# Twenty-four layer norms of a two-layer decoder: where the residual is added, where the statistics are read and which engine applies them

## The chip, the cores and the metric

One core of one Trainium2 chip runs the whole program in one launch. The metric is the device time of that launch in microseconds (us). TensorE (PE) multiplies and writes its results to PSUM. VectorE (DVE) and ScalarE (ACT) read PSUM and SBUF, GpSimd (POOL) reads SBUF, and SyncE (SP) issues the transfers. Each engine works through its own instructions in order and waits on semaphores for the others.

## The reference

The input is two sequences of 1024 tokens with 256 features. Two decoder layers follow, each with three sublayers, and after each sublayer stands a layer norm without affine terms:

```
def _layernorm(x, axis=-1, eps=1e-05):
    m = jnp.mean(x, axis=axis, keepdims=True)
    v = jnp.var(x, axis=axis, keepdims=True)
    return (x - m) / jnp.sqrt(v + eps)

x = _layernorm(x + _L0_attn_ref(...))    # recurrent mixer (scan over 1024 steps), then 32 -> 256
x = _layernorm(x + _L0_xattn_ref(...))   # cross attention to 77 context rows, 16 heads
x = _layernorm(x + _L0_ffn_ref(...))     # entmax-gated experts, 256 -> 1024 -> 256
x = _layernorm(x + _L1_attn_ref(...))    # self attention, 16 heads of 64
x = _layernorm(x + _L1_xattn_ref(...))   # cross attention
x = _layernorm(x + _L1_ffn_ref(...))     # blockwise FP4 gate/up/down, 256 -> 704 -> 256
```

All arithmetic of the norms is in float32.

## The kernel before

The program runs in stages one after the other: `project` and `scan` (the recurrent mixer), `first_layer` (its stage name is `one`), `self_attention` (`self`), and `second_layer` (`two`). The norms stand in `first_layer` and `second_layer` alone.

Both layers are tiled alike. A group is 256 tokens of each of the two sequences; there are four groups, and each engine loops over them by itself, without a barrier between groups. One sequence is one `Chain`, called chain 0 and chain 1 here; it has four PSUM banks of its own and works on two token tiles of 128 (`CTILES = 2`). Each part of a layer is written as a generator for each engine, and `in_turns` takes one step of chain 0, then one step of chain 1, and so on. That fixes the order of the instructions on every engine: a step ends where the code says `yield`, usually just before a wait. Since both chains run the same code, the order is always step i of chain 0, step i of chain 1, step i+1 of chain 0. An engine that waits in a step of chain 1 therefore also holds back the next step of chain 0.

A sublayer ends in products on PE that leave the sublayer's output in a PSUM bank, `y(j)` with 256 columns for token tile j, and a semaphore `y_ready` after the last of the two tiles:

- norm 1 of layer one: line 1114, one product per tile (`wout` by `sqg`)
- norm 2 of both layers: lines 832 and 833, two products with 128 rows each per tile, and one product with a single row that adds the bias `bo`
- norm 3 of layer one: line 976, one product per tile
- norm 1 of layer two: line 1923, eight products per tile (`wo` by `aT`)
- norm 3 of layer two: line 1806, six products per tile, the last with 64 rows

Every such float32 product with 256 columns shows in the trace as two MATMUL records and two LDWEIGHTS records. A transpose (`pe.transpose`, lines 643, 799, 1773, 1799) of 128 columns shows as one.

Class `Norm` (lines 588 to 628) then does, for each chain: DVE adds the residual to the bank and writes x to SBUF (608, two instructions); DVE takes statistics of x (611, two), aggregates them (614, two) and adds epsilon (616, one); POOL raises the variance to the power -0.5 (628, one); DVE subtracts the mean and multiplies (620, two). Each of these is a step of its own, or nearly so. In norm 1 DVE waits ahead of that for `stored`, the store of the last group's x, and for `in_loaded`, the load of the residual `xin`; in norms 2 and 3 the residual is x itself.

After the norms of layer one and after norm 1 of layer two, `Flip` transposes x on PE into bank 2 (643) and copies it to `xT` on ACT (653). After norm 2 of layer two, DVE quantises x (`quantise`, lines 1737 to 1746), and PE transposes the result (1773). After norm 3, SP stores x (1162, 1962). The bias and the query projections are applied by ACT with the same kind of instruction that the change uses (842: `ACT.Identity` with a bias from SBUF).

## Time and profile before

| | |
|---|---|
| Median of three runs | 3557.69 us (3557.44 to 3558.20) |
| The profiled execution's own time | 3557.47 us |
| Its span (first to last instruction) | 3555.5 us |
| PE busy | 2047.1 us (58%) |
| PE weight loads | 1173.9 us (33%) |
| DVE busy | 2272.2 us (64%) |
| ACT busy | 1768.2 us (50%) |
| POOL busy | 611.8 us (17%) |
| Mean granted TensorE clock | 0.70 |

Busy shares are means over the whole program. The stages have different limits: layer one runs from about 1505 to 1990 us of the span and layer two from about 3000 to its end, and a change to the norms can be worth something only there. The granted clock is given as a share of 2.4 GHz: 0.50 is 1.2 GHz, 1.00 is 2.4 GHz.

### The profile page before, as it was taken

The page shows a single profiled execution, that of the slowest core. Times are in us where ns is not written, and L with a number is a line of the kernel's source. Part 1 is how long each engine was busy: PE and PEld are TensorE (multiplying, and loading weights), DVE is VectorE, ACT ScalarE, POOL GpSimd, SP SyncE. Part 2 cuts the span into 40 slices and gives each one's busy share as a digit, 9 for nine tenths or more (in the row PEclk, how much of TensorE's full clock was granted, in tenths as well). Part 3 has the DMA queues.
Part 4 walks back from the last instruction along what each step waited for, and adds up shares of the span by engine and source line. Part 5 has one row for each costly group of instructions (what it writes and reads, how often), then busy time and mean ns, then how long its engine had stood idle before and what let it go on. Part 6 is the DMA issues. An engine that isn't in the chain of part 4 may idle for free. (4 is left out here: it accounts for less than half of the span.)

```text
span 3555.5 us, 43628 instructions
## 1 busy us (share of the span) xinstructions
PE 2047.1 (58%) x10084; PEld 1173.9 (33%) x10084; DVE 2272.2 (64%) x10243; ACT 1768.2 (50%) x5640; POOL 611.8 (17%) x335
## 2 busy tenths in 40 slices
PE   5322222322322222377676599999999983777776
PEld 3222222222222222244443333333333322454453
DVE  3699999999999999743434244554444545444445
ACT  2388888888888888422221244444444441221221
POOL 0000000000000000000000056666666660000000
PEclk8655555555555555567666799999999995777787
DMA  3322222222222222200000100000000002010000
GB/s 80 81 58 53 65 54 52 61 57 53 56 62 53 52 66 52 69 12 24 24 10 1 40 11 14 9 13 16 13 13 9 13 15 81 30 36 6 29 6 6
DMA packets 87805, 129.52 MB, mean 36 GB/s; under 512 B 17572, under 2 KB 64712, under 8 KB 87368
## 3 DMA queue, kind: packets, MB, share of 16 engines
q1 hardware_dynamic: 87624, 127.76, 14.6%
q14 instruction: 147, 1.20, 0.1%
q8 instruction: 34, 0.56, 0.1%
HBM read 103.58 MB, written 23.10 MB: 36 GB/s over the span
## 5 line engine op out<-in xcount | busy, mean ns | idle before, releaser
L541 PE MATMUL scan_acc<-mixer_qbd,scan_flat 128*128 128x4 f32 x1024 | 228.8, 355 | 886.4 <-ACT scan_flat L502 886.4
L513 ACT ACTIVATE scan_cand<-scan_state,scan_cbuf 128x32 f32<-128x32 f32 x2048 | 647.8, 316 | 35.5
L516 ACT ACTIVATE scan_cand<-scan_pre,scan_cbuf 128x32 f32<-128x32 f32 x2048 | 589.0, 288 | 137.8
L1582 DVE TENSOR_REDUCE self_tops<-self_rough 128x2 f32<-128x1024 f32 x256 | 311.5, 1217 | 461.5 <-PE self_rough L1364 461.5
L446 DVE SCALAR_TENSOR_TENSOR scan_prod<-scan_keys,scan_cbuf,scan_cand 128x65 f32<-128x65 f32 x2048 | 585.6, 286 | 18.1 <-issue 8.5
L461 DVE SCALAR_TENSOR_TENSOR scan_pre<-scan_keys,scan_gap,scan_state 128x32 f32<-128x32 f32 x2048 | 527.7, 258 | 36.1
L541 PEld LDWEIGHTS scan_acc<-mixer_qbd,scan_flat 128*128 128x128 f32 x1024 | 223.2, 330 | 912.1 <-ACT scan_flat L502 912.1
L452 DVE SCALAR_TENSOR_TENSOR scan_state<-scan_cand,scan_cbuf 128x32 f32<-128x32 f32 x2048 | 505.0, 247 | 0.0
L1568 POOL TENSOR_TENSOR self_psum<-self_psum,self_prob 128x1024 f32<-128x1024 f32 x192 | 451.2, 2350 | 161.2 <-ACT self_prob L1494 151.8
L628 POOL TENSOR_TENSOR one_norm_rstd<-one_norm_var,one_half 128x2 f32<-128x2 f32 x24 | 18.0, 768 | 1920.0 <-DVE one_norm_var L616 1920.0
L1494 ACT ACTIVATE self_prob<-self_sco 128x1024 f32<-128x1024 f32 x256 | 261.5, 1024 | 137.9 <-PE self_sco L1377 129.3
L1373 PE MATMUL self_sco<-self_qk 64*128 64x512 f32 x1024 | 279.5, 623 | 26.4 <-DMA self_w<-in_w_qkv 22.8
L1388 PE MATMUL self_out<-self_prob,self_v 128*64 128x512 f32 x1024 | 248.8, 607 | 0.0
L532 PE MATMUL scan_flip<-all_ident,scan_state 128*128 128x128 f32 x520 | 126.1, 424 | 100.8 <-DVE scan_state L452 100.8
L446 DVE DVE_READ_ACCUMULATOR scan_prod<-scan_keys,scan_cbuf,scan_cand 128x1 f32 x2048 | 168.9, 82 | 0.0
L502 ACT ACTIVATE scan_flat<-scan_flip 128x128 f32<-128x128 f32 x520 | 138.7, 268 | 1.6 <-PE scan_flip L532 1.6
L1333 PE MATMUL self_misc<-self_xT,self_w 128*128 128x512 f32 x256 | 128.7, 626 | 18.6 <-DMA self_xT<-xT_rows 15.1
L532 PEld LDWEIGHTS scan_flip<-all_ident,scan_state 128*128 128x128 f32 x520 | 101.9, 223 | 105.1 <-DVE scan_state L452 85.9
L1600 DVE RECIPROCAL self_rden<-self_den 128x128 f32<-128x128 f32 x128 | 119.7, 939 | 23.8 <-ACT self_den L1504 23.8
L1373 PEld LDWEIGHTS self_sco<-self_qk 64*128 64x128 f32 x1024 | 93.2, 191 | 116.5 <-issue 101.5
L653 ACT ACTIVATE one_xT<-one_bank 128x512 f32<-128x512 f32 x24 | 14.3, 597 | 229.9 <-PE one_bank L643 229.9
L1485 ACT ACTIVATE self_qk<-self_misc 128x512 f32<-128x512 f32 x64 | 38.2, 597 | 169.1 <-PE self_misc L1333 169.1
(376 smaller groups left out, 3116.4 us busy)
## 6 DMA issues: line engine op xcount, KB each, us to landing
scan_keys<-k_rows SPq DMA_DIRECT2D x260, 260.0 KB, 4.8
aT_rows<-self_aT SPq DMA_DIRECT2D x32, 256.0 KB, 2.4
two_aT<-aT_rows SPq DMA_DIRECT2D x8, 1024.0 KB, 8.0
scan_cbuf<-coef_rows SPq DMA_DIRECT2D x65, 80.0 KB, 5.4
coef_rows<-proj_coef SPq DMA_DIRECT2D x4, 1280.0 KB, 6.0
self_w<-in_w_qkv SPq DMA_DIRECT2D x8, 384.0 KB, 3.5
k_rows<-proj_krow SPq DMA_DIRECT2D x32, 65.0 KB, 3.6
proj_xin<-in_xT SPq DMA_DIRECT2D x8, 256.0 KB, 3.2
```

Source lines behind the costliest of these rows:

```text
L446: dve.scalar_tensor_tensor(prod[:, b, :], keys[:, h, b, s_, :], coef(NIB, h, s_, b), cand[:, b, s % 2, :], ALU.mult, ALU.mult, accum_out=g ...
L452: dve.scalar_tensor_tensor(state[:, h, s_, b, :], cand[:, b, s % 2, 0:NS], weight, cand[:, b, s % 2, NS:2 * NS], ALU.mult, ALU.add).then_i ...
L461: dve.scalar_tensor_tensor(pre[:, b, 0:NS], keys[:, h, b, s_, NS:2 * NS], gap[:, b:b + 1], state[:, hp, sp_, b, :], ALU.mult, ALU.add).the ...
L513: act.activation(cand[:, b, (s + 1) % 2, NS:2 * NS], state[:, hp, sp_, b, :], ACT.Copy, scale=cbuf[:, h, KEEP, b, s_:s_ + 1]).then_inc(kep ...
L516: act.activation(cand[:, b, (s + 1) % 2, 0:NS], pre[:, b, 0:NS], ACT.Tanh, scale=cbuf[:, h, BETA, b, s_:s_ + 1]).then_inc(c_ready[b], 1)
L532: mm = pe.transpose(flip[:, i // 4, (i % 4) * P:(i % 4 + 1) * P], state[:, h, 2 * i:2 * i + 2, :, :].rearrange("p s b j -> p (s b j)"), id ...
L541: mm = pe.matmul(acc[:, at // 512, at % 512:at % 512 + 4], flat[:, i, :], qbd[:, at:at + 4], start=True, stop=True)
L1373: pe.matmul(sco[:, kt % 2, u, :], qk[rows, b, 1, kt * P:(kt + 1) * P], qk[rows, b, 0, hf * HALF:(hf + 1) * HALF], start=True, stop=False)
L1388: mm = pe.matmul(out[u * AD:(u + 1) * AD, :], v[:, b, kt, u, :], prob[:, kt, u, :], start=(kt == 0), stop=(kt == NQ - 1))
L1494: act.activation(prob[:, kt, :, :], sco[:, kt % 2, :, :], ACT.Exp, scale=AD ** -0.5).then_inc(p_ready, 1)
L1568: pool.tensor_tensor(psum[:, hf, :, :], before, prob[:, kt, :, :], ALU.add).then_inc(summed, 1)
L1582: dve.tensor_reduce(tops[:, kh, t, :], rough[:, :, :], AX.X, ALU.max).then_inc(rough_taken, 1)
```

## The change

The residual is no longer added by DVE. PE adds it in the bank: after a tile's products comes one more, `ident` (the 128 by 128 identity) by x of that tile, into the same `y(j)`. PE waits for `in_loaded` in place of DVE. DVE takes its statistics from the bank, and after POOL's power it computes `low` = -mean * rstd in one instruction of two columns. ACT then writes x = rstd * y + low from the bank, two instructions per chain. The wait for the last store moves from DVE to ACT. ACT's list of parts gets the three norms; for each chain a norm's step stands ahead of the flip's.

```
 class Norm:
-    LINKS = 3
+    LINKS = 2
...
+        self.low = ch.sb(name + "_low", [P, CTILES])
...
     def dve(self, dve, g):
         link = ChainLinks(dve, self.links, self.LINKS, g)
-        if self.free:
-
-            yield
-            dve.wait_ge(self.free, g * 16 + 16)
         yield
         dve.wait_ge(self.y_ready, g + 1)
         for j in range(CTILES):
-            ins = dve.tensor_tensor(self.x[:, j, :], self.src[:, j, :], self.ch.y(j, self.bank), ALU.add)
-        yield from link(ins)
-        for j in range(CTILES):
-            ins = dve.bn_stats(self.stats[:, j, :], self.x[:, j, :])
+            ins = dve.bn_stats(self.stats[:, j, :], self.ch.y(j, self.bank))
         yield from link(ins, (self.y_ready, 1))
         for j in range(CTILES):
             ins = dve.bn_aggr(self.mv[:, j, :], self.stats[:, j, :])
...
         dve.tensor_scalar(self.var[:, :], self.mv[:, :, 1], LN_EPS, None, ALU.add).then_inc(self.var_ready, 1)
         yield
         dve.wait_ge(self.rstd_ready, g + 1)
+        dve.scalar_tensor_tensor(self.low[:, :], self.mv[:, :, 0], -1.0, self.rstd[:, :], ALU.mult, ALU.mult).then_inc(self.low_ready, 1)
+        link.close()
+
+    def act(self, act, g):
+        if self.free:
+
+            yield
+            act.wait_ge(self.free, g * 16 + 16)
+        yield
+        act.wait_ge(self.low_ready, g + 1)
         for j in range(CTILES):
-            ins = dve.tensor_scalar(self.x[:, j, :], self.x[:, j, :], self.mv[:, j, 0:1], self.rstd[:, j:j + 1],
-                                    ALU.subtract, ALU.mult)
+            ins = act.activation(self.x[:, j, :], self.ch.y(j, self.bank), ACT.Identity, bias=self.low[:, j:j + 1], scale=self.rstd[:, j:j + 1])
         ins.then_inc(self.ready, 1)
-        link.close()
...
 # CrossAttention.pe (norm 2, both layers)
-            mm = pe.matmul(self.ch.y(j), w.ones[0:1, 0:P], w.bvo[:, 1, :], start=False, stop=True)
+            pe.matmul(self.ch.y(j), w.ones[0:1, 0:P], w.bvo[:, 1, :], start=False, stop=False)
+            mm = pe.matmul(self.ch.y(j), w.ident[:, :], x[:, j, :], start=False, stop=True)
...
 # EntmaxFFN.pe (norm 3, layer one)
-            mm = pe.matmul(self.ch.y(j), self.zT[:, 1, j * P:(j + 1) * P], w.o2[:, :], start=True, stop=True)
+            pe.matmul(self.ch.y(j), self.zT[:, 1, j * P:(j + 1) * P], w.o2[:, :], start=True, stop=False)
+            mm = pe.matmul(self.ch.y(j), self.ident[:, :], x[:, j, :], start=False, stop=True)
...
 # first_layer: Sublayers.pe (norm 1)
                 pe.wait_ge(bo_ready, g + 1)
+                pe.wait_ge(self.in_loaded, g * 16 + 16)
                 for j in range(CTILES):
...
+                    mm = pe.matmul(self.ch.y(j), ident[:, :], self.xin[:, j, :], start=False, stop=True)
...
             def act(self, act, g):
-                for part in (self.flip1, self.xa, self.flip2, self.ff, self.flip3):
+                for part in (self.norm1, self.flip1, self.xa, self.norm2, self.flip2, self.ff, self.norm3, self.flip3):
                     yield from part.act(act, g)
...
             def dve(self, dve, g):
-                yield
-                dve.wait_ge(self.in_loaded, g * 16 + 16)
...
 # Fp4FFN.pe (norm 3, layer two)
+            mm = pe.matmul(self.ch.y(j), w.ident[:, :], x[:, j, :], start=False, stop=True)
...
 # second_layer: Sublayers.pe (norm 1)
                 pe.wait_ge(self.a_loaded, g * 16 + 16)
+                pe.wait_ge(self.in_loaded, g * 16 + 16)
...
+                    mm = pe.matmul(self.ch.y(j, 0), ident[:, :], self.xin[:, j, :], start=False, stop=True)
...
             def act(self, act, g):
-                for part in (self.flip1, self.xa, self.ff):
+                for part in (self.norm1, self.flip1, self.xa, self.norm2, self.ff, self.norm3):
                     yield from part.act(act, g)
```

## Rows read from the trace of the kernel before

**Rows 1.** The page's slices: busy tenths and granted clock, 89 us each.
```profile
PE   5322222322322222377676599999999983777776
DVE  3699999999999999743434244554444545444445
ACT  2388888888888888422221244444444441221221
PEclk8655555555555555567666799999999995777787
```

**Rows 2.** The chain that ended last, layer two, first group: start, us, engine, output, line.
```profile
3068.76 1.15 PE two_bank L833 x2
3069.90 2.01 PE two_bank L832 x4
3071.91 1.16 PE two_bank L833 x2
3073.09 0.75 DVE two_x L608 x2
...
3077.18 0.73 DVE two_x L620 x2
3078.42 0.67 DVE two_q_amax L1737
...
3085.33 1.97 PE two_bank L1773 x8
...
3138.60 14.03 PE two_bank L1923 x64
...
3261.82 13.18 PE two_bank L1806 x48
3274.99 14.03 PE two_bank L1923 x64
```

**Rows 3.** Timeline, norm 1 of layer one, second group: start, us, engine, line, tiles.
```profile
1630.89 3.78 PE L1114 MATMUL one_bank<-one_wout,one_sqg 128*128 128x256 f32 x8 [8.65 <-DVE one_sqg L1221]
...
1634.70 0.75 DVE L608 TENSOR_TENSOR one_x<-one_xin,one_bank 128x256 f32<-128x256 f32 x2 [0.86 <-PE one_bank L1114]
1635.37 1.40 DVE L611 BATCH_NORM_STATS2 one_norm_stats<-one_x 128x6 f32<-128x256 f32 x4
1636.69 0.43 DVE L614 BATCH_NORM_AGGREGATE one_norm_mv<-one_norm_stats 128x2 f32<-128x6 f32 x4
1637.04 0.28 DVE L616 TENSOR_SCALAR one_norm_var<-one_norm_mv 128x2 f32<-128x2 f32 x2
1637.26 1.49 POOL L628 TENSOR_TENSOR one_norm_rstd<-one_norm_var,one_half 128x2 f32<-128x2 f32 x2 [17.01 <-DVE one_norm_var L616]
1637.99 1.54 DVE L620 TENSOR_SCALAR one_x<-one_x,one_norm_mv,one_norm_rstd 128x256 f32<-128x256 f32 x4 [0.66 <-POOL one_norm_rstd L628]
...
1638.77 1.97 PE L643 MATMUL one_bank<-all_ident,one_x 128*128 128x128 f32 x8 [4.11 <-DVE one_x L620]
```

**Rows 4.** Timeline, norm 3 of layer one, second group.
```profile
1735.77 1.89 PE L976 MATMUL one_bank<-one_ff_o,one_ff_zT 128*128 128x256 f32 x8
...
1736.83 1.61 DVE L608 TENSOR_TENSOR one_x<-one_x,one_bank 128x256 f32<-128x256 f32 x4 [0.38 <-PE one_bank L976]
...
1741.76 1.92 PE L643 MATMUL one_bank<-all_ident,one_x 128*128 128x128 f32 x8 [4.10 <-DVE one_x L620]
```

**Rows 5.** Timeline, norm 1 of layer two, second group, and its release by PE.
```profile
3138.53 14.08 PE L1923 MATMUL two_bank<-two_wo,two_aT 128*128 128x256 f32 x64
...
3142.86 1.19 SPq L1962 DMA_DIRECT2D out<-two_x  x2
3146.06 0.75 DVE L608 TENSOR_TENSOR two_x<-two_xin,two_bank 128x256 f32<-128x256 f32 x2 [2.61 <-DMA out<-two_x]
3152.64 0.75 DVE L608 TENSOR_TENSOR two_x<-two_xin,two_bank 128x256 f32<-128x256 f32 x2 [5.83 <-PE two_bank L1923]
```

**Rows 6.** Timeline, the end of the program.
```profile
3548.04 0.75 DVE L608 TENSOR_TENSOR two_x<-two_x,two_bank 128x256 f32<-128x256 f32 x2 [5.21 <-PE two_bank L1806]
...
3551.31 1.54 DVE L620 TENSOR_SCALAR two_x<-two_x,two_norm_mv,two_norm_rstd 128x256 f32<-128x256 f32 x4 [0.65 <-POOL two_norm_rstd L628]
```

**Rows 7.** Groups by form on ACT: busy us, mean ns of one, idle before.
```profile
L653 ACT ACTIVATE one_xT<-one_bank 128x512 f32<-128x512 f32 x24 | 14.3, 597 | 229.9 <-PE one_bank L643 229.9
...
L842 ACT ACTIVATE one_xa_q<-one_bank,one_xa_bqk 128x256 f32<-128x256 f32 x16 | 6.7, 479 | 0.0
...
L846 ACT ACTIVATE one_xa_topT<-one_bank 128x256 f32<-128x256 f32 x8 | 3.1, 384 | 36.0 <-PE one_bank L799 35.8
```

**Rows 8.** Groups by form on DVE in layer one: busy us, mean ns, idle before.
```profile
L620 DVE TENSOR_SCALAR one_x<-one_x,one_norm_mv,one_norm_rstd 128x256 f32<-128x256 f32 x44 | 16.1, 409 | 8.0 <-POOL one_norm_rstd L628 7.2
...
L611 DVE BATCH_NORM_STATS2 one_norm_stats<-one_x 128x6 f32<-128x256 f32 x44 | 15.3, 411 | 0.0
...
L608 DVE TENSOR_TENSOR one_x<-one_x,one_bank 128x256 f32<-128x256 f32 x32 | 12.0, 417 | 47.7 <-PE one_bank L833 45.7 <-PE one_bank L976 1.5
...
L616 DVE TENSOR_SCALAR one_norm_var<-one_norm_mv 128x2 f32<-128x2 f32 x22 | 3.1, 153 | 0.0
```

**Rows 9.** Windows of 1.5 us: busy time of each engine; PEclk is the granted clock.
```profile
3060.00:3061.50 1.50, 1.12 (x3) 0.94 (x4) 0.92 (x2) 0.00 (x0) 0.00 (x0) 0.50 0.00 0
3072.00:3073.50 1.50, 1.06 (x2) 0.34 (x2) 0.41 (x2) 0.00 (x0) 0.00 (x0) 0.50 0.00 0
...
3085.50:3087.00 1.50, 1.50 (x8) 1.40 (x8) 0.38 (x1) 0.52 (x1) 0.00 (x0) 0.50 0.00 0
3090.00:3091.50 1.50, 1.50 (x5) 0.72 (x4) 0.00 (x0) 0.00 (x0) 0.00 (x0) 0.91 0.00 0
...
1643.00:1644.50 1.50, 1.50 (x9) 1.32 (x8) 0.00 (x0) 0.70 (x2) 0.00 (x0) 0.99 0.50 193
```

More of the change, by code:

```diff
@@ L588, with __init__ @@
 class Norm:
-    LINKS = 3
-    def __init__(self, ch, name, src, x, y_ready, half, free=None, bank=3):
-        self.ch, self.src, self.x, self.y_ready, self.half, self.free, self.bank = ch, src, x, y_ready, half, free, bank
+    LINKS = 2
+    def __init__(self, ch, name, x, y_ready, half, free=None, bank=3):
+        self.ch, self.x, self.y_ready, self.half, self.free, self.bank = ch, x, y_ready, half, free, bank
         self.stats = ch.sb(name + "_stats", [P, CTILES, 6])
         self.mv, self.rstd, self.var = ch.sb(name + "_mv", [P, CTILES, 2]), ch.sb(name + "_rstd", [P, CTILES]), ch.sb(name + "_var", [P, CTILES])
-        self.var_ready, self.rstd_ready, self.ready, self.links = (
-            ch.sem(name + "_var_ready"), ch.sem(name + "_rstd_ready"), ch.sem(name + "_ready"), ch.sem(name + "_links"))
+        self.low = ch.sb(name + "_low", [P, CTILES])
+        self.var_ready, self.rstd_ready, self.low_ready, self.ready, self.links = (
+            ch.sem(name + "_var_ready"), ch.sem(name + "_rstd_ready"), ch.sem(name + "_low_ready"), ch.sem(name + "_ready"),
+            ch.sem(name + "_links"))
     def dve(self, dve, g):
         link = ChainLinks(dve, self.links, self.LINKS, g)
-        if self.free:
-            yield
-            dve.wait_ge(self.free, g * 16 + 16)
         yield
@@ L932, in __init__, with pe @@
             sem("h_made"), sem("h_ready"), sem("z2_made"), sem("z2_ready"), sem("y_ready"), sem("links"))
-    def pe(self, pe, g, xT, x_flipped):
+    def pe(self, pe, g, x, xT, x_flipped):
         w, banks = self.w, self.ch.banks
@@ L1098, in __init__ @@
                     ch.sem("in_loaded"), ch.sem("y_ready"), ch.sem("stored"), ch.sem("xT_stored"))
-                self.norm1 = Norm(ch, "norm1", self.xin, self.x, self.y_ready, half, self.stored)
+                self.norm1 = Norm(ch, "norm1", self.x, self.y_ready, half, self.stored)
                 self.flip1 = Flip(ch, "flip1", self.x, self.norm1.ready, self.xT, ident, self.xT_stored)
                 self.xa = CrossAttention(ch, context)
-                self.norm2 = Norm(ch, "norm2", self.x, self.x, self.xa.y_ready, half)
+                self.norm2 = Norm(ch, "norm2", self.x, self.xa.y_ready, half)
                 self.flip2 = Flip(ch, "flip2", self.x, self.norm2.ready, self.xT, ident)
                 self.ff = EntmaxFFN(ch, experts, ident, half)
-                self.norm3 = Norm(ch, "norm3", self.x, self.x, self.ff.y_ready, half)
+                self.norm3 = Norm(ch, "norm3", self.x, self.ff.y_ready, half)
                 self.flip3 = Flip(ch, "flip3", self.x, self.norm3.ready, self.xT, ident)
@@ L1765, in __init__, with pe @@
             sem("hq_ready"), sem("h_flipped"), sem("hT_ready"), sem("y_ready"), sem("links"))
-    def pe(self, pe, g):
+    def pe(self, pe, g, x):
         w, banks = self.w, self.ch.banks
@@ L1805, in pe @@
                 size = min(P, FI - r * P)
-                mm = pe.matmul(self.ch.y(j), self.hqT[0:size, j, r, :], w.wdT[0:size, r, :], start=(r == 0), stop=(r == self.FT - 1))
+                pe.matmul(self.ch.y(j), self.hqT[0:size, j, r, :], w.wdT[0:size, r, :], start=(r == 0), stop=False)
+            mm = pe.matmul(self.ch.y(j), w.ident[:, :], x[:, j, :], start=False, stop=True)
         mm.then_inc(self.y_ready, 1)
@@ L1909, in __init__ @@
                     ch.sem("in_loaded"), ch.sem("a_loaded"), ch.sem("y_ready"), ch.sem("stored"))
-                self.norm1 = Norm(ch, "norm1", self.xin, self.x, self.y_ready, half, self.stored, bank=0)
+                self.norm1 = Norm(ch, "norm1", self.x, self.y_ready, half, self.stored, bank=0)
                 self.flip1 = Flip(ch, "flip1", self.x, self.norm1.ready, self.xT, ident)
                 self.xa = CrossAttention(ch, context)
-                self.norm2 = Norm(ch, "norm2", self.x, self.x, self.xa.y_ready, half)
+                self.norm2 = Norm(ch, "norm2", self.x, self.xa.y_ready, half)
                 self.ff = Fp4FFN(ch, fp4)
-                self.norm3 = Norm(ch, "norm3", self.x, self.x, self.ff.y_ready, half)
+                self.norm3 = Norm(ch, "norm3", self.x, self.ff.y_ready, half)
             def pe(self, pe, g):
@@ L1919, in pe @@
                 pe.wait_ge(self.a_loaded, g * 16 + 16)
+                pe.wait_ge(self.in_loaded, g * 16 + 16)
                 for j in range(CTILES):
                     for c in range(CT):
-                        mm = pe.matmul(self.ch.y(j, 0), self.aT[:, c, j * P:(j + 1) * P], wo[:, c, :], start=(c == 0), stop=(c == CT - 1))
+                        pe.matmul(self.ch.y(j, 0), self.aT[:, c, j * P:(j + 1) * P], wo[:, c, :], start=(c == 0), stop=False)
+                    mm = pe.matmul(self.ch.y(j, 0), ident[:, :], self.xin[:, j, :], start=False, stop=True)
                 mm.then_inc(self.y_ready, 1)
                 yield from self.flip1.pe(pe, g)
-                yield from self.xa.pe(pe, g, self.xT, self.flip1.ready)
-                yield from self.ff.pe(pe, g)
+                yield from self.xa.pe(pe, g, self.x, self.xT, self.flip1.ready)
+                yield from self.ff.pe(pe, g, self.x)
             def act(self, act, g):
-                for part in (self.flip1, self.xa, self.ff):
+                for part in (self.norm1, self.flip1, self.xa, self.norm2, self.ff, self.norm3):
                     yield from part.act(act, g)
@@ L1937, in dve @@
             def dve(self, dve, g):
-                yield
-                dve.wait_ge(self.in_loaded, g * 16 + 16)
                 yield from self.norm1.dve(dve, g)
```

10 lines of the change are left out of this document (5 added, 5 removed).

## The prediction

> **What bounds the kernel now.** I read the page's slices first, to see in which stages the norms stand: no engine is full there (DVE 3 to 5 tenths, PE 7 to 8, ACT 1 to 4), and PE's granted clock is between its two levels [rows 1]. Two chains take turns and each waits for the other engine, so the time of these stages is the length of a chain of waits. The chain that ended last comes next: in layer two it runs through PE's last products for chain 1, then DVE's addition, statistics, POOL's power, DVE's scaling, and on to the quantiser [rows 2]. Between groups it goes over the products of lines 1806 and 1923, which stand back to back on PE [rows 2]. So PE's products ahead of a norm are on the path, all of them, and those of both chains, since chain 1's come after chain 0's. Then the timeline of one norm of each kind, to time each link of it [rows 3 to 6].
>
> Call Y the moment when chain 1's bank is complete (DVE's addition for chain 1 begins). Before, in norm 1 of layer one, Y = 1634.70 and the flip on PE begins at 1638.77: Y + 4.07 [rows 3].
>
> **What is added on PE.** Four identity products per norm (two chains, two tiles), of 256 columns: two records each, so 8 records. At full clock line 1923's 64 records take 14.08, one 0.22 [rows 5]; at 1.2 GHz twice that, 0.43 to 0.44, and line 1114's eight agree (3.78 in all, with the tail of the last) [rows 3]. So 8 records cost 1.75 at full clock and 3.45 at the lower.
> A change between 128-row and one-row products costs more: lines 832 and 833 take 2.0 + 1.15 = 3.15 for six records [rows 2], 0.54 more than 6 x 0.435, with two changes per tile, so 0.27 each. The identity product puts one more such change at the end of norm 2.
> Its bounds: a product as cheap as two transposes, which show one record per 128 columns [rows 3] (half of the above), up to the 0.57 per record of line 833 (4.6 for eight) [rows 2].
>
> **What leaves DVE, and what ACT takes.** After Y, DVE no longer adds, and chain 0's statistics are already done: they wait no more behind chain 1's addition. From Y: chain 1's statistics, two instructions 0.33 apart (four take 1.40 [rows 3], one 0.411 [rows 8]), 0.66; aggregation 0.35; to POOL's start 0.22: POOL begins at Y + 1.23, before at Y + 2.56. The power and its hand-over 0.73 (1637.26 to 1637.99), so DVE's small instruction stands at Y + 1.96. It takes 0.16, like others of two columns (0.153 [rows 8]), and 0.09 to hand over: ACT begins at Y + 2.21. ACT's form with one operand from SBUF took 0.479 for 256 columns, without one 0.384 [rows 7]: an operand costs 0.095, and with a scale from SBUF too I take 0.57. A pair takes about 1.0, so chain 0's x is ready at Y + 3.2 and the flip starts at Y + 3.27. Saved: 0.8. Bounds for the pair: 0.75 (DVE's pair) to 1.2 (twice the 0.597 of a 512-column copy [rows 7]).
> The statistics now read PSUM. The additions that read it took 0.417, the statistics 0.411 and the scaling 0.409 in SBUF [rows 8]; I take nothing for it, 0.05 per norm at most.
> ACT's order: chain 0's pair, chain 1's pair, then chain 0's copy of the flip. Chain 1's pair starts when chain 0's ends (its power is 0.75 later) and ends at Y + 4.2; the flip of chain 0 takes PE until about Y + 4.4 (half of line 643's 1.97 and the hand-over). So the copy isn't held back. The table loads that a function of another set needs have always stood in ACT's idle time ahead of a wait, and the new instruction is of the form of line 842, which runs between the same functions. By the Trainium skill, "ScalarE: Activation LUTs", section "Table sets: the hidden batching unit", identity is in every set, so no load is added; no row here shows Identity right behind Gelu, and one load more in ACT's idle time would cost nothing either.
>
> **Waits that move.** PE waits for `xin`. Behind that wait stand the products of lines 1114 and 1923 and all of PE; but `xin` is requested a group ahead and, in the first group, ahead of `aT`, which PE awaits anyway: nothing. Its bound is the 2.61 that DVE waited for a store [rows 5]. ACT now waits for that store; behind it stand the norm's pair and the flip's copy. The store was issued at 3142.86 and landed at 3146.06, while x is wanted from about 3155 on: hidden. SP's loads wait for norm 1 as before and go out some us later, a group ahead of use. POOL's queue holds only the powers.
>
> **The sum.** Layer one, per group:
> - norm 1, at 1.2 GHz (line 1114): +3.45 - 0.8 = 2.65
> - norm 2, at 1.2 GHz (0.50 from the first to the last window of the same burst in layer two [rows 9]): +3.45 + 0.27 - 0.8 = 2.9
> - norm 3, at full clock: PE starts at 1735.77; 16 records end at 1739.3, Y = 1739.4; flip at 1742.7, before 1741.76 [rows 4]: 0.9
>
> That is 6.45, times four 25.8.
> Layer two:
> - norm 1, groups two to four: 1.75 for its own products, 1.75 and half a change (0.14) for norm 3's products ahead of them on PE, less 0.8: 2.85; the first group 0.95. Together 9.5. The rest of norm 3 lies beside line 1923's 14 us.
> - norm 2: the quantiser needs both chains' x. Before, its second instruction starts at about Y + 5.3 (3078.42 [rows 2]); now chain 1's pair ends at Y + 4.2: 1.1 saved. +3.72 - 1.1 = 2.6, times four 10.4.
> - the last norm 3: +1.9 on PE; chain 1's x was ready at 3552.85 = Y + 4.8 [rows 6], now Y + 4.2: 1.3.
>
> That is 21.2. In all 47.0.
>
> **What the clock gives back.** A dense stretch of PE is granted the full clock after a while: line 1773's transposes and 1785's products start at 3085.3 and are at 0.91 in the window from 3090.0, 5 us on; the flip and the queries start at 1638.8 and are at 0.99 from 1643.0, 4.2 us on [rows 2, 3, 9]. Line 1114's stretch lasted 3.8; with the identity products it would last 7.0, so about its last 2 us run at twice the speed: 0.9 back, times four 3.6. The norm-2 burst is not dense, with its one-row products and the gaps at each change; it was at 0.50 for 12.7 us. I take no rise in it. The Trainium skill ("TensorE: Matmul & The Clock Gate", section "Why this matters for your kernels") says that keeping TensorE busy without a break brings it to the full clock. By that rule the burst should have risen long before; this trace disagrees, at 0.50 throughout. The change adds full-array products to it, and that is the first rival.
> 47.0 - 3.6 = 43.4. The profiled execution took 3557.47, within the runs' own 3557.44 to 3558.20. Forecast: 3557.5 + 43 = **3600**.
>
> **Rivals.**
> A. The clock rises in the norm-2 bursts (other side: not slower). For it: more of the burst will be products of the kind that the risen stretches consist of, six records of eight per tile against four of six. Against: 12.7 us at 0.50 in the trace, while dense stretches rose after 4 to 5. If it rises 5 us into a burst of 16.4, the rest takes half: 10.7, 5.7 back, times eight 46: 3557.5 + 43 - 46 = 3555, from "same" to slightly faster. It decides from a rise in nearly all eight bursts; if PE even enters them at full clock, 8 back each, it is 3537.
> B. ACT takes longer than DVE did. For it: two operands from SBUF, two pairs in series, and chain 0's copy queued behind chain 1's pair. If a pair takes 1.2 and the copy waits 0.5, that is 0.7 at each of 20 norms on the path, +14: 3614. Against: the 0.2 of slack worked out above.
> C. Identity products at half price, as transposes. For it: line 643's records; against: line 976's products, with the same shapes, show two records. Half of 3.45 at the 12 norms at 1.2 GHz (norm 2 of both layers, norm 1 of layer one) is 20, half of 1.75 at eight others 7: 3573.
> D. Rises move. A stretch that starts later may get the full clock at the same moment, which halves its delay, or a step later, which adds to it; the stretches of lines 965, 1785 and 1806 and the flips all hang on it. Up to 1 us per group for each of two stretches: 3600 -+ 16. This is the forecast's own width.
>
> **How the numbers follow.** Forecast with D 0.74, A 0.07, B 0.12, C 0.07. The likeliest case's own range is 3584 to 3614. Of A nothing is taken in; C reaches to 3573, so the low end is 3577, and the high end 3613. A measurement of this kernel can tell about 0.2%, 7 us, from no change. Slower: all but A and a little of the unforeseen, 0.91; same: 0.04; faster: 0.05.
>
> **What would show it.** In the changed profile, line 608's additions and 620's scaling are gone; identity products show as 96 records in each layer, 0.43 apart in norm 2 and 0.22 in line 1923's; ACT's new instructions are 48 in each layer, of 0.57. From the end of PE's last product to the flip's first it is 3.3 instead of 4.1. Norm 2's PE burst is 16.4 long at 0.50: if the clock there is 1.00, A is right. A group of layer two (136.4 between two starts of line 1923's products before [rows 2]) is longer by some 5.5, one of layer one by 5 to 6.5. The mixer, the scan and the self attention keep their durations. I am wrong if the stretch ahead of a norm isn't longer by the identity products, or if the groups grow by less than 3 us.

## The result and the profile after

The changed kernel takes 3574.51 us (median of five runs, 3566.89 to 3577.65), the kernel before 3557.44 on the same chip (3556.40 to 3558.20). The ratio is 1.0047, 95% interval 1.0032 to 1.0062: slower by 17 us (11 to 22). The forecast of 3600 is too slow by 25, and 3574.5 lies just below its range: the direction was right, the size too large. In the experiments below one run of `e2_norms1and3_only` took 6435.67 us; it is left out, and that kernel's median is over its other five runs.

The page after: the line of busy times, and the slices that answer to [rows 1]. Before, PE was busy for 2047.1 us in 10084 records and DVE for 2272.2; 192 records are added, and PE's busy time grows by only 39:

```profile
PE 2086.0 (58%) x10276; PEld 1210.8 (34%) x10276; DVE 2214.8 (62%) x10099; ACT 1815.0 (51%) x5736; POOL 608.5 (17%) x335
...
PE   5322222222222223377667599999999975687776
...
PEclk8655555555555555577676799999999986788787
```

No engine became full: these are still chains of waits. Norm 1 of layer one, second group, answers to [rows 3] (timeline: start, us, engine, line, tiles, then idle time before and what ended it):

```profile
1630.04 1.22 PE L1120 MATMUL one_bank<-one_wout,one_sqg 128*128 128x256 f32 x2 [8.73 <-DVE one_sqg L1226]
...
1631.05 1.06 PE L1122 MATMUL one_bank<-one_xin,all_ident 128*128 128x256 f32 x2
...
1635.65 0.59 PE L1122 MATMUL one_bank<-one_xin,all_ident 128*128 128x256 f32 x2
1636.28 0.76 DVE L606 BATCH_NORM_STATS2 one_norm_stats<-one_bank 128x6 f32<-128x256 f32 x2 [1.66 <-PE one_bank L1122]
1636.96 0.43 DVE L609 BATCH_NORM_AGGREGATE one_norm_mv<-one_norm_stats 128x2 f32<-128x6 f32 x4
1637.31 0.29 DVE L611 TENSOR_SCALAR one_norm_var<-one_norm_mv 128x2 f32<-128x2 f32 x2
1637.54 1.35 POOL L631 TENSOR_TENSOR one_norm_rstd<-one_norm_var,one_half 128x2 f32<-128x2 f32 x2 [18.91 <-DVE one_norm_var L611]
1638.26 0.16 DVE L614 SCALAR_TENSOR_TENSOR one_norm_low<-one_norm_mv,one_norm_rstd 128x2 f32<-128x2 f32 x1 [0.66 <-POOL one_norm_rstd L631]
1638.46 1.93 ACT L625 ACTIVATE one_x<-one_bank,one_norm_low,one_norm_rstd 128x256 f32<-128x256 f32 x4 [14.57 <-DVE one_norm_low L614]
...
1639.53 1.82 PE L646 MATMUL one_bank<-all_ident,one_x 128*128 128x128 f32 x7 [3.29 <-ACT one_x L625]
```

Read it from the statistics on: Y = 1636.28, the power begins at Y + 1.26, ACT at Y + 2.18, the flip at Y + 3.25 (forecast: 1.23, 2.21, 3.27). The stretch of products is 6.2 long instead of 7.0, because its last records run at twice the speed (two take 0.59 instead of 1.06).

Norm 2 of the same group. The kernel before has 24 records here, all at the lower clock (timeline of before, columns as above):

```profile
1678.13 2.07 PE L832 MATMUL one_bank<-one_xa_w,one_xa_aT 128*128 128x256 f32 x4 [4.03 <-DVE one_xa_aT L875]
1680.13 1.22 PE L833 MATMUL one_bank<-one_xa_bvo,all_ones 1*128 1x256 f32 x2
...
1694.90 1.97 PE L643 MATMUL one_bank<-all_ident,one_x 128*128 128x128 f32 x8 [4.10 <-DVE one_x L620]
```

The changed kernel:

```profile
1679.63 2.08 PE L835 MATMUL one_bank<-one_xa_w,one_xa_aT 128*128 128x256 f32 x4 [4.03 <-DVE one_xa_aT L879]
...
1681.63 1.22 PE L836 MATMUL one_bank<-one_xa_bvo,all_ones 1*128 1x256 f32 x2
...
1682.78 1.22 PE L837 MATMUL one_bank<-one_x,all_ident 128*128 128x256 f32 x2
...
1686.58 0.70 PE L837 MATMUL one_bank<-one_x,all_ident 128*128 128x256 f32 x2
...
1690.81 0.70 PE L837 MATMUL one_bank<-one_x,all_ident 128*128 128x256 f32 x2
1691.55 0.76 DVE L606 BATCH_NORM_STATS2 one_norm_stats<-one_bank 128x6 f32<-128x256 f32 x2 [3.47 <-PE one_bank L837]
...
1694.79 2.03 PE L646 MATMUL one_bank<-all_ident,one_x 128*128 128x128 f32 x8 [3.28 <-ACT one_x L625]
```

From the first product to the flip it is 15.16; before, 16.78. The same line's pair takes 1.22 at first and 0.70 from the second tile on. The windows of that burst (1.5 us each: busy time of PE, of its weight loads, of DVE, ACT and POOL, then the granted clock) show why, and below them those of layer two's first and second group, which answer to [rows 9]:

```profile
1684.00:1685.50 1.50, 1.50 (x5) 0.81 (x3) 0.00 (x0) 0.00 (x0) 0.00 (x0) 0.50 0.00 0
1685.50:1687.00 1.50, 1.50 (x5) 0.90 (x5) 0.00 (x0) 0.00 (x0) 0.00 (x0) 0.73 0.00 0
1687.00:1688.50 1.50, 1.50 (x8) 0.95 (x6) 0.76 (x2) 0.00 (x0) 0.00 (x0) 1.00 0.00 0
```
```profile
3075.00:3076.50 1.50, 1.50 (x5) 1.15 (x5) 0.00 (x0) 0.00 (x0) 0.00 (x0) 0.50 0.00 0
...
3214.50:3216.00 1.50, 1.50 (x5) 0.52 (x4) 0.00 (x0) 0.00 (x0) 0.00 (x0) 0.67 0.00 0
3216.00:3217.50 1.50, 1.50 (x8) 1.06 (x7) 0.00 (x0) 0.00 (x0) 0.00 (x0) 1.00 0.00 0
```

So the clock rose in the norm-2 burst: in all four groups of layer one, 6.7 us after its start, and in groups two and four of layer two, 10.3 after it. In groups one and three of layer two it stayed at 0.50. Six of eight.

Norm 3 of layer one (timeline), which answers to [rows 4]: the flip stands 6.90 behind the first product (which starts at 1735.16), before 5.99.

```profile
1742.06 2.03 PE L646 MATMUL one_bank<-all_ident,one_x 128*128 128x128 f32 x8 [3.28 <-ACT one_x L625]
```

Layer two, the last part of norm 3 and norm 1 of the next group. This is the chain that ended last (start, us, engine, output, line), which answers to the same chain of before [rows 2]; the identity products stand in it one by one:

```profile
3131.22 4.14 PE two_bank L1811 x12
3135.35 0.63 PE two_bank L1812 x2
...
3146.22 3.45 PE two_bank L1930 x16
3149.67 0.43 PE two_bank L1931 x2
```

Groups by form (busy us, mean ns of one, idle before), which answer to [rows 7, 8]:

```profile
L625 ACT ACTIVATE one_x<-one_bank,one_norm_low,one_norm_rstd 128x256 f32<-128x256 f32 x48 | 23.2, 563 | 203.3 <-DVE one_norm_low L614 203.3
```
```profile
L606 DVE BATCH_NORM_STATS2 one_norm_stats<-one_bank 128x6 f32<-128x256 f32 x48 | 18.3, 423 | 73.2 <-PE one_bank L837 42.5 <-PE one_bank L1122 21.9 <-PE one_bank L981 8.8
```

ACT's instruction takes 0.563 (forecast 0.57), the statistics from PSUM 0.423 against 0.411 from SBUF.

**Where the time went**, in us, from the first product of a norm to what follows it, before and after:

```
                                          before        after          change  forecast
layer one  norm 1, products to flip       7.7 to 7.9    8.8, then 9.5  +1.5    +1.75 (2.65 - 0.9)
           norm 2, products to flip       16.78         15.16          -1.6    +2.9
           norm 3, products to flip       5.99          6.90           +0.9    +0.9
layer two  norm 3's products to the flip  31.3          34.0           +2.7    +2.85
           norm 2 to quantiser, gr. 1, 3  24.95         27.49          +2.55   +2.6
           norm 2 to quantiser, gr. 2, 4  24.95         24.65          -0.3    +2.6
```

From one flip of norm 3 to the next, a group of layer one is 122.8 long on average, before 121.3. From group two on, the starts of line 1930's products in layer two are 139.6 and 140.3 apart, before 136.4 and 136.5. Two rows of the table went against the forecast's sign, both of norm 2, and in both the clock rose inside the burst.

### The profile page after: what moved, and what is told of

Its sections match the earlier page's. It is cut to its first block and busy times, and to the rows that moved or that the text cites. A ratio compares the mean times of both kernels' runs of the same rounds, so it can differ in the third digit from the quotient of the medians.

```text
span 3572.6 us, 43944 instructions
## 1 busy us (share of the span) xinstructions
PE 2086.0 (58%) x10276; PEld 1210.8 (34%) x10276; DVE 2214.8 (62%) x10099; ACT 1815.0 (51%) x5736; POOL 608.5 (17%) x335
## 5 line engine op out<-in xcount | busy, mean ns | idle before, releaser
L625 ACT ACTIVATE two_x<-two_bank,two_norm_low,two_norm_rstd 128x256 f32<-128x256 f32 x48 | 23.2, 564 | 228.3 <-DVE two_norm_low L614 228.3
L532 PEld LDWEIGHTS scan_flip<-all_ident,scan_state 128*128 128x128 f32 x520 | 102.0, 224 | 105.4 <-DVE scan_state L452 86.1
L1605 DVE RECIPROCAL self_rden<-self_den 128x128 f32<-128x128 f32 x128 | 119.8, 940 | 23.8 <-ACT self_den L1509 23.8
L606 DVE BATCH_NORM_STATS2 two_norm_stats<-two_bank 128x6 f32<-128x256 f32 x48 | 18.3, 423 | 183.5 <-PE two_bank L1812 67.5
```

Source lines behind the costliest of these rows:

```text
L532: mm = pe.transpose(flip[:, i // 4, (i % 4) * P:(i % 4 + 1) * P], state[:, h, 2 * i:2 * i + 2, :, :].rearrange("p s b j -> p (s b j)"), id ...
```

## The experiments

Each was measured (four to eight runs) beside the kernel before on the same chip, whose median was 3565.07 for the first four, 3561.34 for the next four, 3562.65 for the three after and 3559.89 for the last. Differences are of medians, ratios with their 95% interval. Where a kernel keeps some norms as before, `OldNorm` is the class `Norm` of before. "Burst" is the stretch of PE that holds the norm-2 projection.

**The two halves.** `e1_norm2_only`:
```
-self.norm1 = Norm(...)   self.norm3 = Norm(...)      # both layers, without their identity products
+self.norm1 = OldNorm(...)   self.norm3 = OldNorm(...)
```


> Only norm 2 of both layers is changed; norms 1 and 3 are as before. Theory (the identity products let PE's clock rise inside the norm-2 burst, and that gives back more than they cost): the burst of 32 records lasts 11.5 to 13.2 us where the granted clock rises within it and 15.8 where it doesn't; from its start to the flip's start layer one takes about 15.2 against 16.8, and the total is 3551 to 3562. Rival (the clock has no part; the products or the norm's chain are cheaper than reckoned, somewhere in all norms alike): the burst stays at 0.50 and the total is a third to a half of the way from before to the changed kernel, 3563 to 3567; at my own old prices it would be 3579.


Measured 3548.26: 0.9955 [0.9942, 0.9968], 16.8 below before. `e2_norms1and3_only`, the other half:
```
-self.xa = CrossAttention(...)   self.norm2 = Norm(...)
+self.xa = CrossAttention(... as before)   self.norm2 = OldNorm(...)
```


> Only norms 1 and 3 are changed; norm 2 is as before in both layers. Theory: these norms cost what I reckoned (1.7 per group for norm 1 and 0.9 for norm 3 in layer one, 2.8 for both in layer two), and the norm-2 burst is back at 12.05 us at 0.50: 3575 to 3580, as slow as the full change or slower. Rival (all norms cheaper alike): 3567 to 3570.


Measured 3583.54: 1.0050 [1.0037, 1.0063], 18.5 above. In the first all eight bursts rise, 6.2 after their start (6.65 in one), as the windows of one show, and norm 2 is a gain; in the second none rises and 16.80 stands from product to flip, as before.

```profile
1687.20:1688.70 1.50, 1.50 (x4) 0.68 (x3) 0.00 (x0) 0.00 (x0) 0.00 (x0) 0.50 0.00 0
1688.70:1690.20 1.50, 1.50 (x7) 1.08 (x7) 0.03 (x1) 0.00 (x0) 0.00 (x0) 0.92 0.00 0
```

The halves give +2 together and the whole +17. Most of the difference lies in layer two: all its bursts rise early where norms 1 and 3 are old (22.75 to the quantiser), two rise late and two not at all where they are new (24.65 and 27.49), which is 13 us over the four groups.

**Is it the kind of product?** `e3_before_dense_bias` is the kernel before with the norm-2 bias as an identity product against the bias on 128 rows, in place of a one-row product; `e4_change_dense_bias` is the changed kernel with that:
```
-pe.matmul(self.ch.y(j), w.ones[0:1, 0:P], w.bvo[:, 1, :], ...)
+pe.matmul(self.ch.y(j), w.ident[:, :], w.bo[:, :], ...)      # w.bo: loaded on 128 partitions
```


> The kernel before with one edit: in norm 2's burst the bias is added by the identity times a tile that holds the bias in all 128 rows, in place of one row of ones times one row of bias. Same number of records, no identity product for the residual. Theory (what decides is whether the burst's products keep the array busy enough for the clock): the burst of 24 records falls from 12.05 to 7.5-8.7 with the granted clock rising inside it, 4 us at each of eight, total 3522 to 3530. Rival (only the changes between one-row and 128-row products go, the clock stays): 10.0 to 10.4, total 3539 to 3543.


Measured 3517.67: 0.9870 [0.9856, 0.9885], 47.4 below, more than expected: the 24 records take 6.65, not 7.5 to 8.7. Products to flip 11.14 (before 16.78), to the quantiser 19.13 (24.95).


> The changed kernel with the same edit of the bias product. Theory: all eight norm-2 bursts rise, and earlier: 32 records in 9 to 10.5 us against 11.5 in layer one and 13.2 or 15.8 in layer two; total 3545 to 3555. Rival (the rise in the changed kernel has another cause, and only the row changes go): 10.3 and 12 to 13.6, total 3562 to 3568.


Measured 3541.66: 0.9939 [0.9926, 0.9952], 23.4 below; 12.1 and 19.9. The number of records is the same in each pair and only the rows of one product in the burst differ. The windows of one burst of the first kernel:

```profile
1678.20:1679.70 1.50, 1.49 (x4) 1.22 (x5) 0.55 (x1) 0.00 (x0) 0.00 (x0) 0.50 0.00 0
1679.70:1681.20 1.50, 1.50 (x5) 1.23 (x4) 0.00 (x0) 0.00 (x0) 0.00 (x0) 0.50 0.00 0
1681.20:1682.70 1.50, 1.50 (x8) 1.26 (x8) 0.02 (x1) 0.00 (x0) 0.00 (x0) 0.92 0.00 0
1682.70:1684.20 1.50, 1.50 (x8) 1.33 (x7) 0.73 (x2) 0.00 (x0) 0.00 (x0) 1.00 0.00 0
```

The profile shows PE busy in nearly the whole of each, as it does through the burst of before at 0.50, and the clock rises 3.2 after the start. This edit takes two things out of the burst at once: the one-row products, and the changes between the two kinds of product, each of which costs about 0.3 from start to start (four 128-row records and a change take 2.00, where 4 x 0.427 is 1.71).

`e5_change_sparser` goes the other way: the changed kernel with the bias split in two one-row products of 128 columns, one behind each projection product. The one-row columns are as many as in the changed kernel; the changes between the kinds are twice as many, and fewer 128-row records stand in a row (at most four, not six):
```
 for f in range(KT):
     pe.matmul(self.ch.y(j), self.aT[:, f, ...], w.w[:, 3, f, :], ...)
+    pe.matmul(self.ch.y(j)[:, f*P:(f+1)*P], w.ones[0:1, 0:P], w.bvo[:, 1, f*P:(f+1)*P], ...)
-pe.matmul(self.ch.y(j), w.ones[0:1, 0:P], w.bvo[:, 1, :], ...)
```


> The changed kernel with norm 2's bias row split in two products of 128 columns, one behind each of the tile's two other products, so that no more than four records of full products stand between one-row products. All else is the same, the results too. Theory: the granted clock rises in none of the eight bursts; 32 records and 16 pieces of bias take about 17.9 us (15.8 measured without a rise, and 8 more changes of 0.27), and the total is about 55 us above before (17 for the change, 6.4 in each of four bursts of layer one, 2.1 or 4.7 in those of layer two). Rival (the clock in the burst has no part): only the added changes cost, 2.2 in each of eight bursts, 35 above before.


Measured 3621.63: 1.0167 [1.0153, 1.0181], 60.3 above. No burst rises in its whole length; 22.04 from product to flip, 29.8 to the quantiser. A window near the end of one:

```profile
1705.00:1706.50 1.50, 1.50 (x5) 0.68 (x3) 0.00 (x0) 0.00 (x0) 0.00 (x0) 0.50 0.00 0
```

**Take products out of the burst.** Bank 3 is free and x complete long before `aT` is. `e6_change_residual_early` issues the norm-2 identity product there, `e7_norm2_all_early` (norm 2 changed alone) the bias too, and `e8_early_where_idle` is that with norm 1 of layer one and norm 3 of layer two changed and their identity products early as well (the latter into bank 1, behind the transposes of h):
```
 mm.then_inc(self.a_made, 1)
+pe.matmul(banks[3][:, :], w.ident[:, :], x[:, :, :].rearrange("p j c -> p (j c)"), start=True, stop=False)
+pe.matmul(banks[3][:, :], w.ones[0:1, 0:P], bcast(w.bvo[:, 1, :], 1, CTILES), ...)     # e7, e8
...
-start=(f == 0)      # the projection adds to it
+start=False
```


> The changed kernel with norm 2's identity product moved: one product of 512 columns for both tiles, issued behind the attention products, while DVE takes the reciprocals and PE idles; the burst itself holds 24 records as before. Theory: the burst is back at 12.05 us at 0.50 and stays there; from its start to the flip 16.0 (16.8 before, less 0.8), to the quantiser's transposes 23.8; total about 12 above before. Rival (identity products on the path were what cost; the clock has no part): 2.9 per group under the forecast's own price, 8 x 3.7 = 30 under the forecast of 43, so 13 above before - the total can't tell these two, the bursts' clock and lengths can: in the changed kernel 11.5, here 12.05 with 8 records fewer. Third: the early product keeps PE at full clock into the burst, which then takes 6.3: about 35 below before.


Measured 3579.94: 1.0044 [1.0030, 1.0058], 18.6 above, against 12 expected. The burst is the one of before again: at 0.50 throughout in five groups, while in three PE enters it at full clock and the clock falls 0.8 to 1.9 into it. That gives 3.4 back; but the stretches from flip to burst are together 10 longer than in the changed kernel.


> Norm 2 alone is changed, and both its identity product (512 columns for both tiles) and its bias (one row, 512 columns) are issued in PE's idle time; the burst holds only the 16 records of the projection. Theory: 16 dense records at 0.50 would be 6.9 us; a rise after 4 makes them 5.4 to 6; against 12.05 that is 6 to 6.6 less at each of eight, and 0.8 to 1.1 of DVE's chain besides: 54 to 62 below before. If the clock doesn't rise in so short a burst, 5.2 less each: 48 below.


Measured 3515.62: 0.9866 [0.9851, 0.9881], 45.7 below, against 54 to 62 expected. From products to flip or quantiser 66 is saved over the eight groups; from flip to burst 19 is lost.


> The version that the runs point to: norm 2 as in the run before; norm 1 of layer one with its identity product ahead of the wait for the mixer's output; norm 3 of layer two with its identity product in bank 1 while PE waits for the quantiser; norm 3 of layer one and norm 1 of layer two as in the kernel before, since PE has no idle time ahead of them. Expected against the run before: 0.8 less at each of four norms 1 and 0.6 once at the end, so 4 us, give or take what the clock does: 55 to 68 below before.


Measured 3507.36: 0.9845 [0.9832, 0.9858], 54.0 below, against 55 to 68 expected. `e9_bias_early_alone` is the kernel before with only the bias early:
```
 mm.then_inc(self.a_made, 1)
+pe.matmul(banks[3][:, :], w.ones[0:1, 0:P], bcast(w.bvo[:, 1, :], 1, CTILES), start=True, stop=False)
```


> The kernel before with one edit: norm 2's bias (one row, 512 columns) is issued in PE's idle time behind the attention products, with the accumulation group opened there. No identity product; all norms on DVE as before. Theory: the burst is the 16 dense records of the run with both early, 5.0 us and a last record; only the chain of the norm is the old one, 0.8 (layer one) or 1.1 (layer two) longer, so 7 to 8 us above the run with identity and bias early: 37 to 39 below before. Rival (the early identity product keeps PE awake and is what makes that burst short): 5.2 less per burst by the eight records that go, without a rise, 33 below at most, the burst at 6.9.


Measured 3515.89: 0.9868 [0.9853, 0.9883], 46.8 below, against 37 to 39 expected. So moving the one-row product alone is worth as much as everything the seventh kernel does. Products to flip are 10.30 here and 8.69 there, but from the flip to the burst it is 40.9 and 42.3 (39.4 to 40.1 before): chain 0's early products stand in PE's queue ahead of chain 1's attention products. The timeline of the seventh kernel shows who waits for them, two reciprocals that stood back to back before:

```profile
1671.92 1.13 PE L879 MATMUL one_bank<-one_x,all_ident 128*128 128x512 f32 x2
1672.06 3.36 DVE L932 RECIPROCAL one_xa_rden<-one_bank 128x512 f32<-128x512 f32 x1 [15.36 <-PE one_bank L875]
...
1677.75 3.36 DVE L932 RECIPROCAL one_xa_rden<-one_bank 128x512 f32<-128x512 f32 x1 [2.34 <-PE one_bank L875]
```

**ACT's part alone.** `e10_act_scales_no_identity` keeps DVE's addition and the statistics from SBUF, and lets ACT scale from SBUF:
```
-ins = dve.tensor_scalar(self.x[:, j, :], self.x[:, j, :], self.mv[:, j, 0:1], self.rstd[:, j:j + 1], ...)
+dve.scalar_tensor_tensor(self.low[:, :], self.mv[:, :, 0], -1.0, self.rstd[:, :], ALU.mult, ALU.mult)
+ins = act.activation(self.x[:, j, :], self.x[:, j, :], ACT.Identity, bias=self.low[...], scale=self.rstd[...])
```


> The kernel before with ScalarE's part alone: DVE adds the residual and takes the statistics as before, makes the small product, and ACT applies scale and offset, here from x in SBUF; no identity products. By the trace of the changed kernel DVE's small instruction and the hand-over take 0.2 and ACT's pair 1.0 to 1.1 against DVE's 0.78, so each flip starts 0.4 to 0.5 later and the quantiser's second instruction gains nothing: 8 to 11 us above before, more or less by what the clock does. If ACT's part were the gain, it would be 10 to 20 below before.


Measured 3571.72: 1.0025 [1.0015, 1.0036], 9.1 above. Products to flip 17.33 in norm 2 (16.78 before). The move to ACT costs 0.55 a norm by itself (its instruction took 0.589 from SBUF); in the change, where the flip comes 0.8 sooner after Y, the saving is that the addition has gone and the statistics of chain 0 are done ahead of Y.

**The change again**, to see whether the same bursts rise, `e11_change_again` (no edit).


> The changed kernel itself, beside the runs of the kernel before on this chip: between 11 and 22 above before, as at first; norm-2 bursts with a rise in layer one, and in some of layer two's groups.


Measured 3580.73: 1.0041 [1.0027, 1.0055], 18.1 above. All four of layer one rise again, 6.6 to 6.8 after their start; in layer two groups one and three do (10.3 after it), two and four don't, the other way about, with the same two lengths (13.2 and 15.8).

**Early, and behind both chains.** `e12_early_own_step` gives the early products of the eighth kernel a step of their own, so that chain 0's come behind chain 1's attention products:
```
 mm.then_inc(self.a_made, 1)
+yield
 pe.matmul(banks[3][:, :], w.ident[:, :], x[:, :, :].rearrange("p j c -> p (j c)"), start=True, stop=False)
```


> The run with early products where PE idles, with one edit: norm 2's early identity and bias products are a step of their own, so they stand behind the attention products of both chains and not between chain 0's and chain 1's. In the run with norm 2 all early, the way from the flip to the burst was 1.35 us longer than with the bias alone early, and DVE waited 2.3 us for chain 1's attention products ahead of its second reciprocal, which before followed the first without a gap. Theory (chain 0's early products held back chain 1's attention products): the flip-to-burst stretch is back at 40 to 41, at eight norms 1.3 less each, 10 us below that run: 62 to 66 below before. Rival (the longer stretch is where the clock's rises fell): no change, 54 below before.


Measured 3471.32: 0.9750 [0.9736, 0.9763], 88.6 below, against 62 to 66 expected. It is faster than the kernel before by 2.5%, and than the changed kernel, measured on another chip, by 2.9%. The flip-to-burst stretch is back at 38.8 to 40.2, as hoped for. What was not foreseen is in this timeline of its norm 2:

```profile
1663.38 1.12 PE L881 MATMUL one_bank<-one_x,all_ident 128*128 128x512 f32 x2
1663.52 3.36 DVE L934 RECIPROCAL one_xa_rden<-one_bank 128x512 f32<-128x512 f32 x1
...
1666.54 1.12 PE L883 MATMUL one_bank<-one_xa_bvo,all_ones 1*128 1x512 f32 x2
1666.79 1.22 DVE L935 TENSOR_TENSOR one_xa_aT<-one_bank,one_xa_rden 128x512 f32<-128x512 f32 x2
...
1667.59 3.72 PE L888 MATMUL one_bank<-one_xa_w,one_xa_aT 128*128 128x256 f32 x16
...
1674.59 2.03 PE L693 MATMUL one_bank<-all_ident,one_x 128*128 128x128 f32 x8 [3.27 <-ACT one_x L625]
```
```profile
1667.00:1669.00 2.00, 2.00 (x9) 1.25 (x8) 1.01 (x2) 0.00 (x0) 0.00 (x0) 1.00 0.00 0
```

PE has no idle time in front of the burst, where before it waits 4.03 for `aT`, and the clock, which in the kernel before falls in that wait, stays at 1.00 through all eight bursts: 16 records in 3.7. Products to flip 7.0, to the quantiser 14.81 (before 16.78 and 24.95). The same wait in the kernel before, its two windows ahead of the burst at 1678.13:

```profile
1674.00:1676.00 2.00, 0.10 (x4) 0.00 (x0) 1.90 (x2) 0.00 (x0) 0.00 (x0) 1.00 0.00 0
1676.00:1678.00 2.00, 0.00 (x0) 0.00 (x0) 2.00 (x3) 0.00 (x0) 0.00 (x0) 0.79 0.00 0
```

This accounts for the size: (16.78 - 7.0) x 4 + (24.95 - 14.81) x 4 = 79.7 of the 86.1 between the two profiled spans (3555.5 and 3469.4). The rest is norm 1 of layer one, 6.8 to 7.1 against 7.7 to 7.9 (3.6 over four groups), and smaller pieces. Against the eighth kernel, from which it differs by the one `yield`, about 18 comes from the stretches between flip and burst and 13 from the bursts, of 39.5 between the two profiled spans.

## Why the prediction was wrong

**The step that failed** is "I take no rise in it", of the norm-2 burst, and with it the chance of 0.07 for rival A. The burst rose in six of eight groups. Against the forecast's +2.9 in layer one stands -1.6, 4.5 lower, times four; against +2.6 in layer two stands -0.3 in two groups, 2.9 lower. That is 23.8, and 43.4 - 23.8 = 19.6, against the 17.1 measured. The remaining 2.5 are within what the stretches between the norms vary by: from flip to burst it was 39.8 in layer two and is 38.6 or 40.2, for example. A sign that the prediction had named for being wrong came true as well: a group of layer one grew by 1.5, less than 3. That the kernel still came out slower, as forecast, hung on layer two: where all eight bursts rose, in the first experiment, norm 2 gained 16.8, and with the other half's 18.5 that would have been no measurable change.

The prediction's reading of the burst before, "not dense, with its one-row products and the gaps at each change", isn't refuted: the third experiment takes both away, and all eight bursts rise. What was wrong was to carry "no rise" over to a burst with another mix. The bursts below are all entered behind a wait of 4.03, with the clock at its lower level from the first product on or at most 0.11 later:

```
kernel                        a tile's products (rows)             rises after (us)
before with 128-row bias      128, 128, 128                        2.8 to 3.3
change with 128-row bias      128, 128, 128, 128                   2.8 to 3.5
norm 2 alone changed          128, 128, 1, 128                     6.2, one 6.65
the change                    128, 128, 1, 128                     6.7; 10.3 or never in layer two
before                        128, 128, 1                          never (12.05 long)
change, bias split            128, 1, 128, 1, 128                  never (18.1 long)
```

A burst with one-row products counts as busy in the profile and stays at the lower clock, or rises later, all the same. By swapping that one product the third and fourth experiments show that this product is the cause. Which property of it counts isn't shown: its single row, the 0.3 at each change to and from it, or how few full products stand between two of them. The fifth experiment adds changes at the same number of one-row columns, and all eight bursts lose their rise, so the single row can't be the whole of it. The Trainium skill ("TensorE: Matmul & The Clock Gate", section "Why this matters for your kernels") says to keep TensorE busy without a break for the full clock; the trace bears that out for products on all rows, and disagrees for the bursts with one-row products, which the profile shows busy for 12 us at 0.50. I had seen this disagreement before the run and drew from it that the rule doesn't hold for this burst, where I should have asked what the change does to the thing that makes it fail: three products of full height to one of one row, in place of two to one. Its rise had to be looked for between the "never" of the burst before and the 4.2 to 5 us of the stretches in [rows 9], with a chance nearer to a half.

Rival A itself had the mechanism right and the size too large: it took a rise 5 us in, in all eight, for 5.7 each; it was 6.7 in for 4.5 each, and in layer two 2.9 each in two.

**The terms that held.** Layer one's norm 1: 1.5 for 1.75 (1.7 in groups two to four), the rise at its end included. Norm 3: 0.9 for 0.9. Layer two: norm 1 with norm 3's products 2.7 for 2.85; norm 2 without a rise 2.55 for 2.6. The 0.8 saved on the chain: the flip came at Y + 3.25 for 3.27. The second experiment adds these terms up alone: 4 x (1.75 + 0.9) + 9.5 + 1.3 = 21.4 from the forecast's rows, and it measured 18.5. Rival B didn't come: ACT's pair took 1.0, and PE waited 0.20 (its weight load in norm 3) for chain 1's x. Rival C didn't: two records for each identity product, 96 in each layer. Rival D's part can be seen, in layer one's steadier groups and layer two's alternating ones, and is within the 16 that it was given. The wait of ACT for `out` stayed hidden. The table load of layer two's ACT moved from the flip's copy to line 625 (four loads as before), in idle time.

**What orders the rises, and what isn't settled.** The same instructions rise early, late or not at all, and the traces show with what this goes: with the moment at which the clock falls, counted from the burst's start. Over the 24 bursts with this mix (the change, its repeat and norm 2 alone), the clock fell 0.03 to 0.63 ahead of the burst's start in 16, and all of them rose, 6.2 to 6.8 after the start; it fell 0.01 to 0.11 after the start in four, and these rose at 10.3; it fell 1.5 ahead in four, and these didn't rise. The groups that rise in the repeat and not at first, and the other way about, follow this too. The windows around the start of layer two's first (3063.41) and second burst (3205.21) in the changed kernel:

```profile
3060.40:3061.80 1.40, 0.00 (x0) 0.00 (x0) 1.40 (x1) 0.00 (x0) 0.00 (x0) 1.00 0.00 0
3061.90:3063.30 1.40, 0.00 (x0) 0.00 (x0) 1.40 (x3) 0.00 (x0) 0.00 (x0) 0.50 0.00 0
...
3203.80:3205.20 1.40, 0.00 (x0) 0.00 (x0) 1.40 (x3) 0.00 (x0) 0.00 (x0) 1.00 0.00 0
3205.30:3206.70 1.40, 1.40 (x4) 1.08 (x4) 0.45 (x1) 0.00 (x0) 0.00 (x0) 0.50 0.00 0
```

So for this mix a few hundredths of a microsecond can lie between a rise at 6.8 and one at 10.3, and the rows of before don't say where the fall will be. The other mixes don't change their outcome in this way: in the burst of before (its own run and the second and tenth experiment, 24 bursts) the clock fell from 1.1 ahead to 0.12 after, and it never rose; with a 128-row bias (16 bursts) it fell from 0.57 ahead to 0.10 after, and it always rose within 3.5. Why the fall comes at different moments of an equally long wait, and why so small a shift decides, no run tells. Nor does the time waited order the rises: the ninth kernel's burst, all of 128-row products behind a wait of 2.97, rose at 5.0 (its clock had fallen 1.8 ahead), the third's behind 4.03 at 3.2 (fallen 0.2 ahead).

## What to carry to other kernels

Count a product not by its time alone but by what it does to the clock of the stretch around it: with a full-height product in place of the one-row bias product of the norm-2 burst, or with that product moved elsewhere, this kernel gained 47 us, more than the 37 that its records took (8 x 4 x 1.15). Products that don't depend on the late operand (bias, residual) belong in PE's wait for it, queued behind everything that another engine waits for; in the last experiment, with norm 3 of layer one and norm 1 of layer two left as before, this filled the wait and kept the clock up: a gain of 2.5%, where the change as it stood lost 0.5%. When a trace contradicts a rule about the clock, find what in that stretch makes the exception, see whether the change touches it, and if it does, give the rise a chance of its own.

## What the runs showed of the hardware

- A burst that the profile shows busy throughout stayed at 1.2 GHz for 18 us (the fifth experiment, all eight bursts) with one-row products mixed in; with 128-row products in their place it reached 2.4 GHz 2.8 to 3.5 after its start (the third and fourth).
- The full clock was kept over the wait for DVE by four 512-column products, two of them of one row (1.06 from start to start at 2.4 GHz), that left no idle time before the burst (the last experiment). In the seventh kernel, where PE had waited 1.92, the clock fell 0.4 to 1.1 into the burst and rose again 3.8 to 4.5 after its start.
- Statistics from PSUM cost 0.423 for 256 columns, 0.012 more than from SBUF; ACT with scale and offset from SBUF 0.563 reading PSUM.
